# Two key tiles' lower halves made by one GpSimd instruction in a conv-attention kernel

## The reference

```python
xn = group_norm(x)                       # 32 groups
q, k, v = Wq @ xn, Wk @ xn, Wv @ xn      # 8 heads of 64
attn = softmax(q^T k)                    # over 2304 keys, per head
out  = attn @ v
y = x + gamma * out + Wsc @ xn
```

## Time and profile before

| | |
|---|---|
| device time, median of 3 runs | 3122.6 us (3122.47 to 3123.22) |
| profiled execution, first to last instruction (span) | 3120.7 us |
| TensorE busy | 3078.5 us, 99% |
| TensorE weight loads | 2183.3 us, 70% |
| VectorE busy | 2284.6 us, 73% |
| ScalarE busy | 2244.3 us, 72% |
| GpSimd busy | 2787.6 us, 89% |
| granted TensorE clock, mean | 0.998 |

### The profile page before, as it was taken

One profiled execution on the slowest core, in us unless ns is written; L12 is line 12 of the kernel. 1 busy time (PEld: TensorE's weight loads), 2 busy tenths in 40 slices (PEclk: granted clock), 3 DMA queues, 4 the chain that ended last, 5 costly groups with the idle time before them and its releaser, 6 DMA issues.

```text
span 3120.7 us, 119616 instructions
## 1 busy us (share of the span) xinstructions
PE 3078.5 (99%) x52307; PEld 2183.3 (70%) x52307; DVE 2284.6 (73%) x3624; ACT 2244.3 (72%) x4020; POOL 2787.6 (89%) x2039
## 2 busy tenths in 40 slices
PE   6999999999999999999999999999999999999998
PEld 4677777767777677777777777777776777767766
DVE  7777777777787777777777777777777777777774
ACT  5676787777676777777667677778776767667676
POOL 1788999999898899999889899999988989889899
PEclk9999999999999999999999999999999999999999
DMA  3111110110112011110112111111101010101011
GB/s 130 31 40 39 30 47 23 45 34 23 36 40 59 20 38 41 27 53 25 24 33 57 40 29 41 38 31 46 23 25 24 22 27 20 29 20 28 21 29 30
DMA packets 168968, 110.78 MB, mean 35 GB/s; under 512 B 120320, under 2 KB 166400, under 8 KB 168448
## 3 DMA queue, kind: packets, MB, share of 16 engines
q1 hardware_dynamic: 168448, 103.13, 12.6%
HBM read 56.10 MB, written 18.87 MB: 24 GB/s over the span
## 4 chain that ended last, share of the span: by engine, by line
PE 91%; POOL 5%; ACT 0%; issue 0%; DVE 0%; ACTq 0%; DVEq 0%
PE SL L441 25%; PE PJ L380 19%; PE MX L413 11%; PE OB L465 10%; PE OB L462 9%; PE OB L464 9%; PE PJ L377 6%; POOL PLO L954 5%; PE SL L436 1%; ACT PE L558 0%; POOL half L950 0%; ACT L676 0%; DVE mx L753 0%; DVE PLO L923 0%; PE SL L389 0%
## 5 line engine op out<-in xcount | busy, mean ns | idle before, releaser
L954 POOL TENSOR_TENSOR PLO<-PE 128x768 f16<-128x768 f32 x1727 | 2551.0, 1500 | 266.8 <-ACT PE L558 255.5
L558 ACT ACTIVATE PE<-SL 128x768 f32<-128x768 f32 x1728 | 1307.3, 809 | 27.6 <-PE SL L441 27.5
L462 PE MATMUL OB<-V,PE 128*128 128x65 f16 x10368 | 1048.5, 193 | 6.8 <-POOL PLO L954 5.7
L464 PE MATMUL OB<-V,PE 128*128 128x64 f16 x10368 | 1048.5, 193 | 0.0
L465 PE MATMUL OB<-V,PLO 128*128 128x65 f16 x10368 | 1048.2, 196 | 0.0
L462 PEld LDWEIGHTS OB<-V,PE 128*128 128x128 bf16 x10368 | 965.1, 99 | 58.2 <-POOL PLO L954 11.7
L441 PE MATMUL SL<-QK 64*128 64x384 f16 x10368 | 1000.8, 323 | 0.1
L464 PEld LDWEIGHTS OB<-V,PE 128*128 128x128 bf16 x10368 | 962.5, 97 | 42.9
L566 ACT ACTIVATE MXC<-MX 128x384 f32<-128x384 f32 x864 | 423.3, 490 | 752.2 <-PE MX L413 752.2
L465 PEld LDWEIGHTS OB<-V,PLO 128*128 128x128 f16 x10368 | 963.4, 98 | 0.0
L753 DVE TENSOR_REDUCE mx<-MX 128x2 f32<-128x768 f32 x864 | 828.4, 959 | 84.4 <-PE MX L413 38.0
(11 more groups left out here) (105 smaller groups left out, 1237.9 us busy)
## 6 DMA issues: line engine op xcount, KB each, us to landing
gx<-x SPq DMA_DIRECT2D x36, 768.0 KB, 4.7
xr<-x SPq DMA_DIRECT2D x96, 192.0 KB, 2.4
out<-xr SPq DMA_DIRECT2D x96, 192.0 KB, 1.9
X<-x SPq DMA_DIRECT2D x6, 768.0 KB, 8.5
CR<-c SPq DMA_TRANSPOSE x96, 2.4
back<-half SPq DMA_TRANSPOSE x95, 2.8
QK<-wk SPq DMA_DIRECT2D x1, 1024.0 KB, 12.7
QK<-wv SPq DMA_DIRECT2D x1, 1024.0 KB, 13.4
```

What stands on the lines that cost most here:

```text
L462: pe.matmul(acc, upper, v[:, D:V1], start=k == 0 and h == 0 and i == 0, stop=False, skip_group_check=True)
L464: pe.matmul(acc[:, 0:D], upper, v[:, 0:D], start=False, stop=False, skip_group_check=True)
L558: act.activation(PE32[:, s % PB, :].rearrange("p (h n) -> p h n", h=2), SL[s % 2][:, :, 0:CH], ACT.Exp, scale=1.0 / SS).then_inc(s_exp, 1)
L954: nc.gpsimd.tensor_tensor(PLO[:, s % PB, :], PE32[:, s % PB, :], PE32[:, s % PB, :].bitcast(BF16)[:, 1:4 * CH:2], ALU.subtract).then_inc(s ...
```

## The change

GpSimd's two `split` instructions of a slot become one over both tiles. It waits for both exponentials and raises `s_rest` once. TensorE's `weigh` waits for the count of its slot in place of its step. The very last step keeps its own path over VectorE, and the step before it is still done alone.

```diff
                 if s + 1 < STEPS:
-                    pe.wait_ge(s_rest, s + 1)
+                    pe.wait_ge(s_rest, s // 2 + 1)
                 else:
                     pe.wait_ge(s_restd, 1)
...
-            def split(s):
-                pool.wait_ge(s_exp, s + 1)
-                nc.gpsimd.tensor_tensor(PLO[:, s % PB, :], PE32[:, s % PB, :],
-                                        PE32[:, s % PB, :].bitcast(BF16)[:, 1:4 * CH:2],
+            def split(s, tiles):
+                pool.wait_ge(s_exp, s + tiles)
+                both = PE32[:, s % PB:s % PB + tiles, :].rearrange("p t n -> p (t n)")
+                nc.gpsimd.tensor_tensor(PLO[:, s % PB:s % PB + tiles, :].rearrange("p t n -> p (t n)"), both,
+                                        both.bitcast(BF16)[:, 1:4 * CH * tiles:2],
                                         ALU.subtract).then_inc(s_rest, 1)
...
-                    split(s)
-                    if s + 2 < STEPS:
-                        split(s + 1)
+                    split(s, 2 if s + 2 < STEPS else 1)
```

## The result

The changed kernel takes 3182.9 us (median of 4 runs, 3182.0 to 3184.9) against 3122.7 us before (4 runs): a ratio of 1.0193, 95% interval 1.0179 to 1.0208. It is slower by 60 us; the forecast was 3193 us, in a range of 3150 to 3460.

A forecast was written before the change was run, and what follows sets the result against it. TensorE, busy 99% of the span, was taken as the bound, GpSimd only in the last block. Slot 1 (31.5), slot 8 (18) and last block (21) summed to 70.5 us more: 3193 us, range 3150 to 3460.

The forecast's parts named there:

- D: Duration of GpSimd's merged instruction over 1536 columns: taken as 2.74 us, between bounds of 2.58 and 2.89 us.
- Start delay and release: Exponentials' end to merged instruction's start, 0.08 us; its end to the weight load of `weigh`, 0.05 us.
- Slot 1: Needs 2.87 us against a stretch of 2.52: TensorE waits 0.35 us, 31.5 us over 90 chunks.
- Slot 8: More GpSimd instructions stand ahead, so the merged one comes 0.21 us late, more with normalization pieces: 18 us in all.
- Last block: Chunks go from 27.2 to some 30.7 us, 21 us more, the split halves no longer overlapping the exponentials.
- The circle over two slots: Last block: weigh, scores, exponentials, merged split, weigh take 3.75 + 2.87 = 6.62 us over two slots.
- L741: Slots 3 and 5: VectorE's L741 starts first, merged instruction 0.35 us longer, covered by spare time; chance 0.55.
- the rival: GpSimd starts before L741 in slots 3 and 5: 1.4 us wait twice a chunk, 246 us, 3436 us total; chance 0.33.
- the 0.58 us spare: Slot 3 and its like: stretch of 3.45 us against 2.87 needed, so no loss if GpSimd comes on time.
- The other side: Rival: last block gains from merging, chunks falling from 27.2 to 24.4 us, some 3106 us total; chance 0.03.
- Group statistics: The few instructions in three chunks are covered and cost nothing; under 1 us each time if slot 4's cover fails.
- The signs: Expected profile: merged instruction 2.74 us (3.09 in slots 3, 5), GpSimd busy some 82%, weight-load waits about 70 us.

The follow-up runs named there:

- the run with the fill: Changed kernel plus a tiny VectorE fill and a wait for it ahead of each L741, so L741 starts behind the merged instruction: 3429.7 us, ratio 1.0984.

## Why the prediction was right, point by point

- **D.** Taken 2.74 us, from the cost of a four-column instruction; measured 2.747. The other end, 2.58, took the slope between 384 and 768 columns, and was the wrong one: the 384-column form reads other types. Which of the differences counts no run tells. The figure for two-input instructions of the Trainium skill (GPSIMD Engine Reference, section 3.1, about 2.6 cycles an element) would have given 3.3 us as an estimate; the trace has 2.75, and the measurement decides.
- **Start delay and release.** 0.08 and 0.05 us, both as measured (1028.10 to 1028.17; 1030.92 to 1030.97).
- **Slot 1.** Forecast 0.35 us late, 31.5 us in all. It is 0.36 late at the weight load, but the next slot gives back 0.15. With chunks 8, 32 and 56 the net is 35.5 - 13.7 = 21.8 us, of which those three are 3.3 (1.56 less 0.46 each) and the others 18.5. The step "The next slots don't give that back, since TensorE has no gaps" was wrong: the weight load had a lead over the matmuls of 0.17 us, a cover that I had not looked for.
- **Slot 8.** Forecast 0.21 us late in the chunk worked out, measured 0.23 (the merged instruction of chunk 84 runs to 2828.38, the weight load is at 2828.43); with the pieces of normalization 0.60 in a chunk of the fullest kind, where I had about 0.5. Gross 20.9 against 18, net 12.6 for the same reason as in slot 1.
- **Last block.** Forecast 21 us, measured 26.9; a chunk takes 31.3 us where I had 30.7. The circle over two slots was right in kind. Its own part is 3.6 us and not 3.75 in the changed kernel (in chunk 92 from slot 1's weight load at 3059.72 to the end of slot 3's exponentials at 3063.31), as the lead of the weight load is gone there too. What I missed is in slot 5: I took L741 to stand in the last block as it does in the others, but L722 comes ahead of it there, so there the rival was true, five times. Slot 5 of the block alone grew by 10.0 us, though how much of that is L741 no run separates.
- **L741.** VectorE goes first in 178 of 190 cases, by less than 0.1 us, the merged instruction is 0.40 us longer there (I had 0.35), and the 0.58 us spare covers it. The forecast stood on this at 0.55 to 0.33, and the run with the order turned shows that the rival's price was right as well. The rule of the Trainium skill (SBUF, "Who interferes with whom") that the second of the two waits for the whole instruction of the first is what the runs show: 0.61 us or 3.08.
- **The other side.** The last block did not gain; its circle, not GpSimd's work, became the bound. No row spoke for a D under 2.4, and none came.
- **Group statistics.** The sum put them at nothing. They cost 4.5 us: 3.3 in slot 1 (above), where it is ScalarE's square root and table loads that shorten the stretch, and 1.2 in slot 4 (1.6, less 0.4 in slot 5), where it is GpSimd's small instructions, 0.54 us in each of the three chunks.
- **The signs.** The merged instruction and L741 took about the durations named (2.747 and 3.15 us, 0.609). GpSimd's busy share fell to 84% (forecast 82%), and the waits of the weight loads grew to 95.8 us (forecast about 70). 66.7 of these stand before 2960 us, where 35.7 us were lost: the part that the lead of the weight loads hides counts in them.

Sum: 21.8 + 12.6 + 26.9 and the 1.2 in slot 4 make 62.5 us, where I had 70.5: the first two terms too large by 15 us, the last and the small one too small by 7. The mechanism was the forecast's, but that the time came within 10 us of it is partly luck: the errors of the terms stand against each other, and the one order of starts on which 246 us hung was decided by 0.06 us.

## What to carry to other kernels

Merging two instructions joins their waits as well: the one waits for the later input, and its consumer for the later output, and this costs wherever the stretch between producer and consumer is shorter than the merged duration, whatever the engine saves. So measure that stretch slot by slot, the shortest one, and compare it with start delay + new duration + release; a mean busy share says nothing of it. And where two engines shut each other out, a longer instruction turns the order of two starts into a risk of its whole length.

## What had not been expected of the hardware

- VectorE's two-input instruction and GpSimd's subtraction were decided by the order of starts down to about 0.1 us: 0.07 us ahead, VectorE takes 0.61 us and GpSimd 3.15; 0.08 us behind, VectorE takes 3.08 us and GpSimd 2.75. In the changed kernel 178 of 190 fall the one way, in the run with the fill 181 the other.
- TensorE's first weight load of a group stood 0.16 to 0.17 us ahead of its matmul while earlier matmuls ran (the slots 1 of the kernel before), so a wait of up to about 0.15 us there cost nothing.
- A GpSimd subtraction saves only 0.14 us by merging two of 768 columns into one of 1536 (2.747 against 2.89 us).
